# A transformer layer's attention loop with the two kinds of score products exchanged in each half step

## What is computed

```python
x = L0_attn_x
xn = _layernorm(x, axis=-1)
x = x + attn(xn, w_qkv, w_out) + ffn(xn, w_gate, w_up, w_down)
# attn, for each of 4 sequences and 16 heads of width 16:
q, k = _rope(q), _rope(k)
scores = jnp.einsum('blhd,bmhd->bhlm', q, k) * scale
attn = jax.nn.softmax(scores, axis=-1)
out = jnp.einsum('bhlm,bmhd->blhd', attn, v).reshape(B, L, D)
return jnp.einsum('bld,ed->ble', out, w_out)
# ffn: (silu(xn @ wg.T) * (xn @ wu.T)) @ wd.T
```

## Time and profile before

| what | value |
|---|---|
| median of 3 runs | 3058.35 us (3058.14 to 3059.47) |
| the profiled execution | 3054.89 us, span 3053.1 us |
| mean granted TensorE clock | 0.985 |
| busy share of the span | TensorE 95%, VectorE 90%, ScalarE 81%, GpSimd 14% |
| reductions for maxima (L1222) | 2048 of 1214 ns |
| exponentials (L828) | 4096 of 597 ns |
| DMA | mean 45 GB/s |

### The profile page before, as it was taken

One profiled execution on the slowest core, in us unless ns is written; L12 is line 12 of the kernel. 1 busy time (PEld: TensorE's weight loads), 2 busy tenths in 40 slices (PEclk: granted clock), 3 DMA queues, 4 the chain that ended last, 5 costly groups with the idle time before them and its releaser, 6 DMA issues.

```text
span 3053.1 us, 67192 instructions
## 1 busy us (share of the span) xinstructions
PE 2898.7 (95%) x27416; PEld 1057.6 (35%) x27416; DVE 2743.3 (90%) x3214; ACT 2467.2 (81%) x4609; POOL 429.4 (14%) x672
## 2 busy tenths in 40 slices
PE   4989898799999999999999999999999999999999
PEld 3555555233333333333323333333333333333336
DVE  6767676999999999999999999999999999999952
ACT  4454545399999999999999999999999999999972
POOL 3454545000000000000000000000000000000000
PEclk9999999699999999999999999999999999999999
DMA  2223232011111111111111111111111111111115
GB/s 93 88 77 101 77 109 72 28 28 31 31 31 30 30 30 31 32 32 32 31 31 31 32 31 31 30 30 30 30 30 30 31 30 31 31 30 30 31 61 173
DMA packets 124599, 137.12 MB, mean 45 GB/s; under 512 B 43264, under 2 KB 103296, under 8 KB 124288
## 3 DMA queue, kind: packets, MB, share of 16 engines
q1 hardware_dynamic: 124288, 132.79, 15.4%
HBM read 88.15 MB, written 34.08 MB: 40 GB/s over the span
## 4 chain that ended last, share of the span: by engine, by line
PE 78%; ACT 7%; DVE 6%; POOL 3%; issue 3%; DMA 0%; ACTq 0%; SPq 0%; POOLq 0%; DVEq 0%
PE psum L699 35%; PE psum L659 19%; PE psum L717 16%; ACT probs L828 5%; PE psum L569 3%; PE psum L642 2%; PE psum L592 2%; POOL qk_rot L873 2%; DVE row_max L1222 1%; POOL parts L879 1%; ACT silu L772 1%; DVE y_blk L1143 1%; ACT staged L779 1%; PE psum L584 1%; DVE rot_s L1121 1%
## 5 line engine op out<-in xcount | busy, mean ns | idle before, releaser
L1222 DVE TENSOR_REDUCE row_max<-psum 128x1 f32<-128x1024 f32 x2048 | 2335.8, 1214 | 51.0 <-PE psum L659 51.0
L828 ACT ACTIVATE probs<-psum 128x512 f32<-128x512 f32 x4096 | 2178.3, 597 | 193.6 <-PE psum L717 94.2
L699 PE MATMUL psum<-probs,v_op 128*32 128x256 f32 (+1 forms) x15872 | 1296.4, 398 | 0.0
L717 PE MATMUL psum<-q_op,k_op 51*128 51x512 f16 x4096 | 862.9, 381 | 31.5 <-ACT probs L828 23.3
L659 PE MATMUL psum<-k_op,q_op 48*128 48x512 f16 x4096 | 806.9, 391 | 24.9 <-DVE row_max L1222 20.5
L659 PEld LDWEIGHTS psum<-k_op,q_op 48*128 48x128 f16 x4096 | 196.4, 93 | 895.5 <-issue 526.3
L699 PEld LDWEIGHTS psum<-probs,v_op 128*32 128x32 f32 x15872 | 312.5, 108 | 526.7 <-issue 497.8
L717 PEld LDWEIGHTS psum<-q_op,k_op 51*128 51x128 f16 x4096 | 371.8, 94 | 273.8 <-ACT probs L828 73.6
L941 POOL TENSOR_TENSOR acc_sb<-acc_sb,inv_rows 128x512 f32<-128x512 f32 x64 | 81.6, 1275 | 1914.9 <-DMA inv_rows<-inv_dram 1914.9
L765 ACT ACTIVATE parts<-qk_rot 128x512 f16<-128x512 f32 x64 | 40.3, 630 | 235.7 <-POOL qk_rot L873 235.7
L569 PE MATMUL psum<-xnT,w 128*128 128x512 f16 x768 | 188.2, 393 | 8.3 <-DVE h L1134 8.3
(11 more groups left out here) (102 smaller groups left out, 972.5 us busy)
## 6 DMA issues: line engine op xcount, KB each, us to landing
qk_dram<-staged SPq DMA_DIRECT2D x64, 256.0 KB, 3.1
q_op<-qk_dram SPq DMA_DIRECT2D x128, 128.0 KB
k_op<-qk_dram SPq DMA_DIRECT2D x128, 128.0 KB
x_ln<-in_x SPq DMA_DIRECT2D x16, 512.0 KB, 4.0
x_res<-in_x SPq DMA_DIRECT2D x16, 512.0 KB, 5.0
y_dram<-y_blk SPq DMA_DIRECT2D x16, 512.0 KB, 3.2
k_op<-qk_dram SPq DMA_DIRECT2D x128, 64.0 KB
q_op<-qk_dram SPq DMA_DIRECT2D x128, 64.0 KB
```

What stands on the lines that cost most here:

```text
L699: mm = pe.matmul(bank(7)[32 * j:32 * j + 32, n0:n1], v_op[:, h % 2, t, :], probs[:, g3 % PROBS, j * BANK + n0:j * BANK + n1], start=(t == ...
L717: pe.matmul(bank(b), k_op[r:e, h % SLOTS, t * P:(t + 1) * P], q_op[r:e, h % SLOTS, j * BANK:(j + 1) * BANK], start=True, stop=True).then_i ...
L828: nc.scalar.activation(probs[:, g2 % PROBS, j * BANK:(j + 1) * BANK], bank(b), ACT.Exp, scale=to_score).then_inc(s2_used, 1)
L1222: nc.vector.tensor_reduce(row_max[:, hl % 2, t, half:half + 1], psum[:, 2 * half * BANK:(2 * half + 2) * BANK], AX.X, ALU.max).then_inc(s1 ...
```

## The change

In each half step the two matmuls for exponentials now come first, then the two for maxima, then the half product. Before, the maxima's came first. Nothing is added or removed, and the waits of each matmul are the same. At the turning step the turn stands ahead of the exponentials' matmuls as before, and so now also ahead of the maxima's half 0.

```diff
@@ step(c, i) of the tensor engine
-            if c < N1:
-                max_half(c, i, 0)
             h = head_of(c, STAB_AT)
...
             for j in range(4):
                 if j == 2:
+                    if c < N1:
+                        max_half(c, i, 0)
                     weigh_v(0)
-                    if c < N1:
-                        max_half(c, i, 1)
                 if 0 <= g2 < N1:
...
+            if c < N1:
+                max_half(c, i, 1)
             weigh_v(1)
             if c > N1:
                 project(c - N1 - 1)
```

## The result

| | before | changed |
|---|---|---|
| median | 3058.40 us (3058.14 to 3059.47, 4 runs) | 3082.27 us (3079.11 to 3085.51, 4 runs) |
| ratio | | 1.0077, 95% interval 1.0060 to 1.0095 |
| profiled execution, span | 3054.89, 3053.1 us | 3079.82, 3078.0 us |
| mean TensorE clock | 0.985 | 0.986 |

The account below looks back on a forecast made before the run. VectorE's reductions, 1.133 us apart, were taken as the bound; 0.46 us lost at the turning step less a little at the first product gave 0.43, times 62, together 27 us: median 3085.5 us, range 3068 to 3104.

Parts of the forecast that it names:

- the turning step: Step after each joined maximum: maxima's pair waits behind the second exponentials' matmul, pause 0.78 us, next half's reduction 0.46 us later.
- the turn: TensorE's work after GpSimd's last piece, which hangs on VectorE alone: still 1.84 us after the joined maximum.
- The bound: Within a head VectorE's reductions set the pace, 1.133 us apart, with TensorE just ahead except at two pauses.
- The even half steps: Half steps away from the two pauses: same joints in either order, again 1.12 us, cost 0.
- The rival of the exposed ring: Ring's wait no longer hidden under maxima: both half steps 1.14 us, 0.2 us more a head, 3098 us; chance 15%.
- The pauses: VectorE's waits: 0.78 us after two reductions behind the joined maximum, then 0.17 and 0.40 us at the first product.
- The sum: Loss over the attention: 62 x 0.43 = 26.7 us, with the first head's 0.2 together 27 us.
- first-product step: Step with the wide product: two pauses make 0.57 us against 0.59 before, reduction 0.43 us later in all.
- ScalarE's stream between the two places is fixed by E: From turning to first-product step, exponentials' matmuls set ScalarE's times: 1518.72 against 1518.73 us, so bank 7's copy stays.
- The rule on tilings: Changing tiling mode drains TensorE, 0.20 us; one change fewer a head would gain 12.6 us; the sum counts nothing.
- The rival of TensorE's own work: Path runs through TensorE, not VectorE: 0.20 us saved ahead of the turn, 12.6 us gain, 3046 us; chance 5%.

Follow-up runs that it names:

- E2: Not a run: the third of a step's four single matmuls for exponentials, in its second half step.
- E3: Not a run: the fourth and last of a step's single matmuls for exponentials; at the first-product step it waits for ScalarE.
- the fastest kernel: Kernel before, wide product ahead of the last exponentials' matmul in first-product steps, half product between the first two exponentials' matmuls in turning steps: 3010.24 us, 0.9849.
- E1: Not a run: the second of a step's single matmuls for exponentials; at the turning step it waits for ScalarE's copy.
- E0: Not a run: the first of a step's four single matmuls for exponentials.

## Why the prediction was right, and where its reason was not

**The bound** was read rightly for 20 of a head's 32 reductions: from the first product to the next joined maximum VectorE runs at 1.133 us without a recorded pause in both kernels. Between the two pauses it runs at 1.133 as well, but there its pace is not what counts, since the stretch ends in a wait for TensorE. The turn follows the joined maximum by 1.84 and 1.85 us in the two kernels, as forecast.

**The even half steps** cost nothing, as said: M to M is 1.11 and 1.14 us by turns in the changed kernel's trace (1528.57, 1529.68, 1530.82), as it was before, and its reductions stand 1.133 apart. The rival of the exposed ring does not show in the trace.

**The pauses** came out nearly to the hundredth: 0.79, 0.17 and 0.40 us against 0.78, 0.17 and 0.40 forecast, 0.45 us in the traced head against 0.43, 0.427 on average. The sum of 62 x 0.43 = 26.7 us stands against 26.9 measured between the joined maxima; medians differ by 23.9 us and profiled executions by 24.9. The forecast of 3085.5 lies 3.2 us above the median, at the upper end of the changed kernel's runs. The idle time before the reductions, 600 to 2900 us, rose from 47.5 to 68.0 us and not to 75; of the pauses only what is idle by the record counts in it.

**The step that failed is the division of the sum**: "0.46 us later" for the turning step, and a first-product step that gives 0.03 back. The times at which each reduction starts were right, and with them the total; that is no luck, since they were followed through to the first product. But reading them as the cost of the step in which they stand was wrong. Put into the turning steps alone, the order costs 0.21 us, not 0.46; put into the first-product steps alone, 0.24, not nothing; and taken out of the turning steps of the changed kernel it gives back 0.06. What I had not done is to ask which of the late events the next thing depends on. The reduction behind the turn was late by 0.46 us, but the next pause, at the first product, would have absorbed it: there VectorE waits for M, whose time follows from E2, and my own working had put E2 at the same time as before (1518.72 and 1518.73). The 0.43 us were made behind E3. "ScalarE's stream between the two places is fixed by E" was right, but it is TensorE's row that paces it up to shortly ahead of the copy: one more pair in that row, with the new order in the turning steps alone, made it 0.22 us longer.

**The rule on tilings.** One change of tiling less in the turning step brought nothing, as the row of T had it: T waits for GpSimd in both kernels, and longer now (0.57 us idle). GpSimd's last piece ends at 1516.85 and at 1525.36 us in the two traces and T starts 0.10 us behind it in both, with M 0.42 us ahead of T in the one and TensorE idle in the other; so the 0.42 us of rows 6 do not measure a change of tiling, and no run here shows the 0.20 us that the prediction took from them. **The rival of TensorE's own work** falls in the form in which it stood, since that gain did not come; but half of its idea was right: TensorE's row is on the path, in the first and the third part and in most of the second.

## What to carry to other kernels

Where an engine pauses tells when it was served late, not what made it late: before a delay is charged to the step in which it shows, follow the path from one repeated event to the next and ask at each joint what the next start depends on; a delay that runs into a later pause of the same engine is free, until that pause is filled. In a loop of engines that work in order, an instruction that stands in its engine's wait for another is free, and the same instruction behind the wait costs its whole length, so the place to look for gains is the longest wait in front of an instruction and what, further down the same queue, does not depend on it: one product moved ahead of one waiting matmul was worth 1.1%. When two edits are judged by their sum, run each alone, and look at the seams that this makes: the new order in the turning steps alone cost 0.21 us a head for a pair that the whole change does not have there. And a timeline that draws a run of instructions as one line does not say that they are back to back: their distance from start to start has to be held against the shortest one seen.

## What the runs showed of the hardware

A single matmul left over from a pair can share its time with the first of the next pair, if that uses the other row group. In the fastest kernel E1 and the next M start together at 1501.92 us, and E1, M and E, five matmuls, take 0.75 us up to the next product (1502.67). But that is as much as three whole pairs take in a row (0.22 + 0.22 + 0.31), and E0 alone ahead of the half product took 0.32 us (1501.03 to 1501.35), as much as a pair: splitting a pair costs the time of one more pair, and pays here only because it is done inside a wait. In the changed kernel the weights of M behind the late E1 cost nothing: M starts at 1526.13, 0.01 us behind E1's weight load.

An activation of 128 x 512 values from PSUM is recorded as 0.60 us long and costs 0.48 us from start to start when ScalarE has its input at hand (1526.83 to 1527.30); a reduction of 128 x 1024 values is 1.21 us long and costs 1.133.
